# A two-layer gated graph network with a neighbour sum on one core: the state's copy moved from DMA to ScalarE, one quad multiplied earlier, x issued by ScalarE

## The reference, cut to what matters

```python
h = x                                        # (4096, 64)
for W, wih, whh, bih, bhh in layer1, layer2:  # the gated graph layers
    m = adj @ (h @ W)                        # adj: (4096, 4096) float32, 64 MB
    gi, gh = m @ wih.T + bih, h @ whh.T + bhh
    r, z = sigmoid(i_r + h_r), sigmoid(i_z + h_z)
    n = tanh(i_n + r * h_n)
    h = relu((1 - z) * n + z * h)
x1 = layernorm(x + h)
mask = adj != 0                              # then, per row of adj:
w = 0.5 ** (number of later neighbours)      # only the last 100 neighbours
out = layernorm(x1 + w @ (x1 @ weight) + bias)
```

## Time and profile before

| | |
|---|---|
| three timed runs | 373.66, 374.5, 375.15 us; median 374.5 |
| the profiled execution | 372.16 us, of which the span is 370.4 us |
| PE busy | 340.7 us, 92% |
| DVE busy | 294.7 us, 80% |
| ACT busy | 173.8 us, 47% |
| granted clock of PE | 0.995 |
| DMA moved | 116.34 MB, mean 314 GB/s |

### The profile page before, as it was taken

How to read it: one execution, slowest core, us unless ns; L and a number is a source line. 1 busy time by engine, 2 the same in 40 slices (tenths; PEclk the granted TensorE clock), 3 DMA queues, 4 the chain that set the end, 5 groups by cost and what they waited for, 6 DMA issues and landing times.

```text
span 370.4 us, 6473 instructions
## 1 busy us (share of the span) xinstructions
PE 340.7 (92%) x2414; PEld 155.7 (42%) x2422; DVE 294.7 (80%) x472; ACT 173.8 (47%) x206; POOL 23.9 (6%) x32
## 2 busy tenths in 40 slices
PE   4996979999999999999999989999898989899982
PEld 1431313333333333333333324444454544679982
DVE  1488978698896777879885569979696999798983
ACT  0003302013031220574593228674969696887992
POOL 1000000000000000000000010202020202002242
PEclk9999999999999999999999999999999999999998
DMA  7999999999999999999999999999999997100011
GB/s 226 407 402 377 408 379 409 368 410 396 373 408 365 401 304 378 375 361 336 313 362 364 357 381 408 355 387 280 399 334 408 319 406 251 30 3 4 2 58 59
DMA packets 36079, 116.34 MB, mean 314 GB/s; under 512 B 4176, under 2 KB 8528, under 8 KB 36048
## 3 DMA queue, kind: packets, MB, share of 16 engines
q1 hardware_dynamic: 36048, 115.92, 84.8%
HBM read 113.81 MB, written 1.05 MB: 310 GB/s over the span
## 4 chain that ended last, share of the span: by engine, by line
PE 55%; DMA 16%; ACT 11%; DVE 9%; issue 7%; POOL 1%; SPq 1%; POOLq 0%; ACTq 0%; DVEq 0%
PE m_acc L456 29%; DMA stream<-in_adj_t 13%; PE out L456 13%; ACT codes L721 4%; PE out L561 3%; DVE run L917 3%; DMA hx<-in_x_pairs 2%; PE rz_ps L534 2%; PE m_acc L561 2%; ACT wexp L721 2%; PE rz_ps L520 2%; PE rz_ps L513 1%; PE n_ps L513 1%; ACT stream L721 1%; PE n_ps L561 1%
## 5 line engine op out<-in xcount | busy, mean ns | idle before, releaser
L456 PE MATMUL m_acc<-stream,s_in 128*64 128x512 f32 x512 | 127.5, 608 | 8.4 <-DMA stream<-in_adj_t 6.0
L873 DVE TENSOR_SCALAR codes<-stream 128x1024 uint8<-128x1024 f32 x117 | 76.9, 686 | 14.5 <-DMA stream<-in_adj_t 14.5
L456 PE MATMUL out<-stream,s_mid 128*64 128x512 f32 x264 | 66.8, 595 | 2.1 <-DMA stream<-in_adj_t 1.8
L456 PEld LDWEIGHTS m_acc<-stream,s_in 128*64 128x64 f32 x512 | 32.9, 137 | 74.3 <-issue 48.3
L456 PE MATMUL m_acc<-stream,s_mid 128*64 128x512 f32 x248 | 57.0, 599 | 3.5 <-DMA stream<-in_adj_t 3.5
L814 POOL TENSOR_TENSOR rstd<-var,mhalf 128x4 f32<-128x4 f32 x16 | 22.0, 1377 | 342.9 <-DVE var L1027 342.9
L922 DVE SCALAR_TENSOR_TENSOR codes<-codes,run 128x1024 uint32<-128x1024 uint32 (+2 forms) x40 | 40.5, 1011 | 1.4
L917 DVE TENSOR_TENSOR run<-run,codes 128x2048 uint16<-128x2048 uint16 (+2 forms) x39 | 39.1, 1002 | 1.5
L721 ACT ACTIVATE wexp<-codes,code_bias 128x2048 uint16<-128x2048 uint8 x18 | 35.7, 1990 | 0.6 <-PE out L561 0.6
L456 PEld LDWEIGHTS out<-stream,s_mid 128*64 128x64 f32 x264 | 18.5, 137 | 39.3 <-issue 38.6
L456 PEld LDWEIGHTS m_acc<-stream,s_mid 128*64 128x64 f32 x248 | 16.4, 136 | 36.8 <-issue 34.9
(11 more groups left out here) (149 smaller groups left out, 404.1 us busy)
## 6 DMA issues: line engine op xcount, KB each, us to landing
stream<-in_adj_t SPq DMA_DIRECT2D x210, 512.0 KB, 6.6
hx<-in_x_pairs SPq DMA_DIRECT2D x8, 128.0 KB, 8.2
mx<-in_x_t SPq DMA_DIRECT2D x8, 128.0 KB, 6.8
mx<-hx SPq DMA_DIRECT2D x16, 64.0 KB, 5.3
x_res<-in_x_pairs SPq DMA_DIRECT2D x8, 128.0 KB, 5.0
out_nodes<-stream SPq DMA_DIRECT2D x8, 128.0 KB, 1.9
const<-in_consts SPq DMA_DIRECT2D x1, 358.0 KB, 7.8
bias_b<-in_bias SPq DMA_DIRECT2D x1, 128.0 KB, 7.9
```

Of the source, the lines that this page charges most:

```text
L456: last = nc.tensor.matmul(to[D * u:D * (u + 1), :], state[:, t * D:(t + 1) * D], stream[:, n % SLOTS, u * CW:(u + 1) * CW], start=start[u] ...
L873: nc.vector.tensor_scalar(edges(p // 2, b, 2 * (p % 2), 2), stream[:, n % SLOTS, :], 0.0, None, ALU.not_equal).then_inc(mask_made, 1)
```

## The change

ScalarE copies the state into `mx[D:P]` by two activations of 64x256 (`state`); the input `x_t` and the SP transfers `state1` and `state2` are gone. ScalarE also issues x, in four transfers instead of eight, and w1 and consts. The bias has its own semaphore and is loaded at the end of chunk 4, centred in chunk 5. Chunk 1 multiplies quad 0 (pairs 0 and 1) twice, so step 14 of pass 2 loads 14 pairs instead of 16, chunk 1 joins `KEPT`, and `ALONG_PAIRS` has 11 in place of 12 for t = 4 and 5.

```diff
-TRI = (0, 0, 2, 3, 4, 4, 5, 5)
+TRI = (0, 1, 2, 3, 4, 4, 5, 5)
...
-KEPT = range(2, 5)
-M2_BANK = {2: 2, 3: 1, 4: 2, 5: 3, 6: 1, 7: 2}
+KEPT = range(1, 5)
+M2_BANK = {1: 1, 2: 2, 3: 1, 4: 2, 5: 3, 6: 1, 7: 2}
...
-PAIRS = [list(range(NP)), list(range(NP)),
+PAIRS = [list(range(NP)), [2, 4, 3, 5, 8, 9, 10, 11, 6, 12, 7, 13, 0, 14, 1, 15],
...
+X_IN = ((0, 1), (1, 2), (2, 4), (4, 8))
+X_PART = [n for n, (first, end) in enumerate(X_IN) for _ in range(first, end)]
+BIAS_AT = 5
...
-ALONG_PAIRS = {1: 11, 2: 12, 3: 12, 4: 12, 5: 12, 6: 11}
+ALONG_PAIRS = {1: 11, 2: 12, 3: 12, 4: 11, 5: 11, 6: 11}
...
-            def state1(g):
-                if g > 0:
-                    sp.wait_ge(gates_done, g)
-                sp.dma_start(mx[D:P, :], x_t[:, bass.ts(g, CW)]).then_inc(state_in, 16)
...
-                for e in range(2):
-                    sp.dma_start(mx[D:P, e * HW:(e + 1) * HW],
-                                 state_of(g)[e * D:(e + 1) * D, :]).then_inc(state_in, 16)
...
+            def state(g):
+
+                if g < NCH:
+                    act.wait_ge(x_in[X_PART[g]], 16)
+                else:
+                    act.wait_ge(h_made, NCH)
+                if g > 0:
+                    act.wait_ge(gates_done, g)
+                for e in range(2):
+                    nc.scalar.activation(mx[D:P, e * HW:(e + 1) * HW],
+                                         state_of(g)[e * D:(e + 1) * D, :], ACT.Copy)\
+                        .then_inc(state_made, 1)
...
+            load_x(0)
+            act.dma_start(w_1[:, :], w1).then_inc(w1_in, 16)
+            load_x(1)
+            load_x(2)
+            act.wait_ge(xw_done, 1)
+            load_x(3)
+            act.wait_ge(pair_used, 2)
+            act.dma_start(const[:, :], consts).then_inc(consts_loaded, 16)
             act.wait_ge(set_pool, SET_POOL)
+            state(0)
...
                     if q == TANH:
                         tanh(b - 1)
+                        state(b)
...
                 if t < NCH:
                     high(g + 1)
+                    state(g + 1)
                 expand_next(before_square)
                 square(t - 1)
```

More of the change, by code:

```diff
@@ L43 @@
 BLK = KT * CW
-TRI = (0, 0, 2, 3, 4, 4, 5, 5)
-KEPT = range(2, 5)
-M2_BANK = {2: 2, 3: 1, 4: 2, 5: 3, 6: 1, 7: 2}
-M2_AFTER = {4: 2, 6: 3, 7: 4}
+TRI = (0, 1, 2, 3, 4, 4, 5, 5)
+KEPT = range(1, 5)
+M2_BANK = {1: 1, 2: 2, 3: 1, 4: 2, 5: 3, 6: 1, 7: 2}
+M2_AFTER = {3: 1, 4: 2, 6: 3, 7: 4}
 BY_TURNS = [0, 8, 1, 9, 2, 10, 3, 11, 4, 12, 5, 13, 6, 14, 7, 15]
-PAIRS = [list(range(NP)), list(range(NP)),
+PAIRS = [list(range(NP)), [2, 4, 3, 5, 8, 9, 10, 11, 6, 12, 7, 13, 0, 14, 1, 15],
          [0, 4, 1, 5, 8, 9, 10, 11, 6, 12, 7, 13, 2, 14, 3, 15],
@@ L60 @@
          BY_TURNS, BY_TURNS] + [[0, 10, 1, 11, 2, 12, 3, 13, 4, 14, 5, 6, 7, 15, 8, 9]] * 2
-QUADS = [(slice(0, 2), slice(2, 4), slice(4, 6), slice(6, 8))] * 2 + \
+QUADS = [(slice(0, 2), slice(2, 4), slice(4, 6), slice(6, 8)),
+         (slice(1, 3), slice(4, 6), slice(0, 4, 3), slice(6, 8))] + \
     [(slice(0, 4, 2), slice(4, 6), slice(1, 4, 2), slice(6, 8))] + \
@@ L65 @@
     [(slice(0, 2), slice(5, 7), slice(2, 4), slice(4, 8, 3))] * 2
-NEED = [(8, 12, 16)] * 2 + [(8, 15, 16)] * 4 + [(8, 13, 16)] * 2
+NEED = [(8, 12, 16)] + [(8, 15, 16)] * 5 + [(8, 13, 16)] * 2
 TURN = [(0, 10), (0, 11), (0, 12), (0, 13), (1, 10), (1, 11), (1, 12), (0, 14), (0, 15),
@@ L86 @@
 N_EARLY = sum(sum(n.values()) for n in CHAIN_EARLY.values())
-ALONG_PAIRS = {1: 11, 2: 12, 3: 12, 4: 12, 5: 12, 6: 11}
+ALONG_PAIRS = {1: 11, 2: 12, 3: 12, 4: 11, 5: 11, 6: 11}
 FIRST = [NCH * NP, *(NCH * NP + len(TURN) + sum(ALONG_PAIRS[u] for u in range(1, t))
                      for t in range(1, NCH))]
-STATE_AT = [FIRST[1] - 1, *(n + SLOTS for n in FIRST[1:NCH - 1]), len(LOADS)]
 RES_AT = [FIRST[1], *(n + SLOTS + 3 for n in FIRST[1:NCH - 1]), len(LOADS)]
@@ L115 @@
 AGAIN = ["w0", "w1", "m"] + [f"d{i}" for i in range(1, 10)]
-PLACE = {block: ("w0", "w1", "x" if n < 3 * ALONG else "k")[n % 3]
+PLACE = {block: ("w0", "w1", "x" if n < 4 * ALONG else "k")[n % 3]
          for n, block in enumerate(ORDER[:RING])}
@@ L149 @@
               for i in range(SLOTS)}
-PLACE_USED.update({"m": len(LOADS), "x": NCH * NP, "k": USED[2 * NCH - 4] + 1})
+PLACE_USED.update({"m": len(LOADS), "x": NCH * NP, "k": USED[2 * NCH - 3] + 1})
 AT_RZ, AT_N, AT_W2, AT_WT = 0, 2 * P, 4 * P, 5 * P
@@ L189, with build @@
                                    (32, 32), (32, 32))]
-def build(nc, adj_t, x_t, x_pairs, w1, consts, bias, out):
+def build(nc, adj_t, x_pairs, w1, consts, bias, out):
     with ExitStack() as ctx:
@@ L340, in x1b_nodes @@
             return x1b[:, i * KT * D:(i + 1) * KT * D].rearrange("p (k d) -> p k d", d=D)
-        x_in = [sem(f"x_in{i}") for i in range(NCH)]
-        w1_in, consts_loaded = sem("w1_in"), sem("consts_loaded")
+        x_in = [sem(f"x_in{i}") for i in range(len(X_IN))]
+        w1_in, consts_loaded, bias_in = sem("w1_in"), sem("consts_loaded"), sem("bias_in")
         adj_in = [sem(f"adj_in{i}") for i in range(SLOTS)]
@@ L351, in build @@
         m2_copied, m2_kept = sem("m2_copied"), sem("m2_kept")
-        state_in, gates_done = sem("state_in"), sem("gates_done")
+        state_made, gates_done = sem("state_made"), sem("gates_done")
         rz_made = sem("rz_made")
@@ L372, in _ @@
         def _(sp):
-            def load_x(c):
-                at = slice(c * HW, (c + 1) * HW)
-                sp.dma_start(hx[:, at], x_pairs[:, at]).then_inc(x_in[c], 16)
             def load(n):
@@ L408, in load_res @@
                 sp.dma_start(x_res[:, :], x_pairs[:, bass.ts(ch, HW)]).then_inc(x_c_in, 16)
-            sp.dma_start(w_1[:, :], w1).then_inc(w1_in, 16)
-            load_x(0)
             for b in range(NCH):
                 for q in range(NP):
-                    if q == NP - 1:
-                        state1(b)
                     load(b * NP + q)
[L417 to L421, removed]
+                    if b == BIAS_AT - 1 and q == NP - 1:
+                        sp.dma_start(bias_b[:, :, :].rearrange("p k d -> p (k d)"), bias)\
+                            .then_inc(bias_in, 16)
             for n in range(NCH * NP, len(LOADS)):
@@ L424, in _ @@
                 for s in range(NCH):
-                    if n == STATE_AT[s]:
-                        state2(s)
                     if n == RES_AT[s]:
                         load_res(s)
-            state2(NCH - 1)
             load_res(NCH - 1)
@@ L441, in x_w1 @@
             def x_w1(c):
-                pe.wait_ge(x_in[c], 16)
+                pe.wait_ge(x_in[X_PART[c]], 16)
                 if c == 0:
@@ L503, in gates @@
                 pe.wait_ge(m_ready, g + 1)
-                pe.wait_ge(state_in, 16 * (g + 1) if g < NCH else 16 * NCH + 32 * (g - NCH + 1))
+                pe.wait_ge(state_made, 2 * (g + 1))
                 if g > 0:
@@ L722, in expand, with load_x @@
                                      bias=code_bias[:, :], scale=float(P)).then_inc(by_act, 1)
+            def load_x(n):
+                at = slice(X_IN[n][0] * HW, X_IN[n][1] * HW)
+                act.dma_start(hx[:, at], x_pairs[:, at]).then_inc(x_in[n], 16)
+            load_x(0)
[6 more added lines that the diff above has]
+            act.dma_start(const[:, :], consts).then_inc(consts_loaded, 16)
             act.wait_ge(set_pool, SET_POOL)
+            state(0)
             act.wait_ge(set_dve, 3)
@@ L753, in _ @@
             to_s_mid(NCH - 1)
+            state(NCH)
             high(NCH)
@@ L831, in weight_max @@
             def weight_max():
-                dve.wait_ge(consts_loaded, 16 * 2)
+                dve.wait_ge(consts_loaded, 16)
                 nc.vector.tensor_reduce(w_max[0:D, 0:1], w_t[0:D, :], AX_X, ALU.max,
@@ L858, in centre_bias @@
             def centre_bias():
+                dve.wait_ge(bias_in, 16)
                 nc.vector.tensor_reduce(stat[:, 0, :], bias_b[:, :, :], AX_X, ALU.add)\
@@ L990, in _ @@
                         constants()
+                    if b == BIAS_AT and q == 13:
                         centre_bias()
@@ L1164 @@
         "adj_t": adj_t,
-        "x_t": np.ascontiguousarray(nodes),
         "x_pairs": np.ascontiguousarray(
```

## The result

The changed kernel takes 369.12 us (median of 4 runs, 368.94 to 371.42) against 374.08 for the kernel before in the same comparison (4 runs): ratio 0.9885, 95% interval 0.9858 to 0.9911, so 4.3 us faster (3.3 to 5.3). A later comparison, with six runs of it, gives 369.34 us and 0.9851 (0.9822 to 0.9879), 5.6 us faster (4.5 to 6.7). The forecast was 5.1 us faster, 369.4 us.

What follows compares the result with a forecast made beforehand. Transfers bound up to 76 us, then PE, transfers again in the turn, then a DVE and ACT loop. Terms −4.0 − 1.3 − 0.4 + 0.6 sum to −5.1 us, 369.4 us from 374.5; whole range 366.9 to 372.1.

Steps and rivals of the forecast that it cites:

- x_t, 3.1 us: Chunks 0 to 2 of pass 1: dropping three x_t transfers, slowed rates plus bytes, gains 3.1 us.
- Rival A: Bytes alone count: low rates stay and SP's issue time was covered; 1.9 us gained, 372.6 us; chance 0.12.
- Bias and start, 1.2 us: Start and chunk 0: first load issued earlier gains 0.9 us, bias leaving chunk 0 gains 0.3 us.
- Quad 0, −0.3 us: Chunk 1: two second multiplications just fit under transfers, costing 0.3 us; two loads saved in pass 2 give 0.
- Pass 1, 4.0 us: Pass 1: PE enters the regime it bounds itself 4.0 us earlier, from 3.1 + 0.3 + 0.9 − 0.3.
- forecast sign: Pass 1: PE's last wait for a load should come about 4 us earlier.
- Turn, 1.3 + 0.4 us: Turn: without SP's state transfers PE gains 1.3 us up to step 8's node matmul, 0.4 more behind it.
- 240.2 of the forecast: After the turn: step 10's first gate operation on DVE at about 240.2 us in place of 245.87.
- t = 7, 0.6 us back: Pass 2, t = 7: nothing covers ScalarE's pair of state copies, so it costs 0.6 us, full length.
- Sum: Whole kernel: −4.0 − 1.3 − 0.4 + 0.6 = −5.1 us, giving a median of 369.4 us.
- Rival C: Pass 2: all seven pairs of copies exposed, 8.3 us against 5.7 of gain, slower at 377.1 us; chance 0.04.
- Rival D: Pass 2 shrinks with its loads, about 3.2 MB less, 8 us, giving 366.5 us; chance 0.06.

Runs made afterwards that it cites:

- first execution of before: The kernel before the change, unchanged, in its first profiled execution: 372.16 us, span 370.4 us, turn 48.08 us.
- second execution of before: The kernel before the change, unchanged, profiled once more: span 372.1 us, turn 49.20 us.

## Why the prediction was right, and where its steps were not

- **x_t, 3.1 us: 2.83 measured**, by the step's own mechanism. A transfer costs its bytes and more than as much again; four extra ones give 0.86 to 1.02 us each, against the 1.0 that the rows of before gave. Rival A is out.
- **Bias and start, 1.2 us: 1.73.** The term was mis-sized. The step counted one earlier first issue; the rate in 3 to 9 us rose as well. Some 0.7 us of the gain have no cause that the runs show.
- **Quad 0, −0.3 us: 0.** The −0.29 between the two executions is chance: 0.26 of it arises in chunk 0, where the kernels do not differ. Its saving in pass 2, 0, holds.
- **Pass 1, 4.0 us: 4.38** against the first execution of before, the same for both of the changed kernel, and 4.86 against the second. PE's last wait for a load in pass 1 ends at 66.86 us in place of 76.44, 9.6 us earlier where the forecast sign was 4.
- **Turn, 1.3 + 0.4 us: 0.8 to 1.1.** This is the step that was furthest off. The mechanism holds (two transfers of the state lower the rate among queued loads), but I had counted nearly all of PE's waits as given back; in the changed kernel it still waits three times for loads, 0.9 us in all. That DVE would bound the gain behind it holds: at the node matmul of step 9 PE now waits 0.99 us for `h_c`. The profile pair alone shows 0.1 us for the whole turn, and the first gate operation of step 10 on DVE at 241.41 us instead of the 240.2 of the forecast; against the second execution of before the turn gained 1.2 us. What single executions show here is largely chance.
- **t = 7, 0.6 us back: 0.95**, or 1.64 in an execution in which the clock falls. A pair takes 0.87 us of ScalarE's time, not the 0.65 of the sum: the second copy starts 0.44 us after the first, which takes 0.41, so that the 0.1 us of overlap taken from other rows is not there. The prediction named the chain from `square` to the sigmoid rightly, and did not see that PE can take its place when it runs at the lower clock.
- **Sum.** With the measured terms it is −4.38 − 0.8 to −1.1 + 0.95 = −4.2 to −4.5 us, against −5.1. Timed, the first comparison gives 4.3 us (3.3 to 5.3), which holds both sums; the second gives 5.6 (4.5 to 6.7), which holds the forecast and the measured terms only at its edge. The terms erred both ways: pass 1 was forecast 0.4 us too small, the gain of the turn less the price of t = 7 some 1.0 to 1.3 us too large. That the forecast of 369.4 stands nearer to the measured 369.12 us than its parts do is in part luck.
- **Rival C** (slower) would have needed all pairs exposed at 0.82 us or more. The price is there, 0.87, but only t = 7 is exposed: sigmoids of t = 5 and 6 are still 17.79 us apart (278.83 and 296.62). **Rival D** falls by the same rows: with 3.1 MB less in all the loop is no shorter.

## What to carry to other kernels

Price a small transfer among queued loads by the rate around it, not by its bytes: one that reaches half of the partitions cost 2.6 to 3.1 times its bytes here, and one to all partitions just its bytes. Before two profiles are compared, look which stages repeat, and where a difference arises: equal passes 1 ended within 0.35 us of each other, the turn, bound by transfers and buffers, spread by 1.8, and the 0.29 us of quad 0 were there before quad 0 was reached. When an operation moves onto a busy engine, look for the place where that engine already waits: put there, the copies gave back two thirds of their price.

## What the runs showed of the hardware that was not expected

- With 64 partitions as their destination, transfers of 128 KB lowered the rate of 3 us from 411 to between 328 and 339 GB/s, at a DMA share of 1.04 and 1.05, upper and lower half alike.
- The granted clock fell to 0.50 behind PE's wait for `h_c` in t = 7 in four of nine executions with a wait of 1.95 to 2.33 us, in none of four with 1.26 to 1.66 us, and in one (in t = 8) with 2.75 us. The same program with the same wait did it once and once not. What else decides is open. One fall of 3.4 us cost 0.65 us at the end of t = 7 beside the copies, and 1.65 without them.
- Two copies of 64x256 from SBUF to SBUF on ScalarE take 0.85 us together (414 ns each, the second 440 ns after the first), with no overlap.
